# Graph attention and experts on one core: in the edge loop the row of destinations is fetched ahead of the list issues

## The reference

```python
hh = (x @ W).reshape(n, H, D)                       # 8 heads of 32
scores = leaky_relu(s_src[src] + s_dst[dst], 0.2)
e = exp(scores - segment_max(scores, dst)[dst])
alpha = e / segment_sum(e, dst)[dst]
out = segment_sum(hh[src] * alpha[:, :, None], dst) + x
x = x + elu(layernorm(out) * gamma + beta)          # graph part
topk_vals, topk_idx = top_k(layernorm(x) @ gate_w + gate_b, 2)
moe = sum_k softmax(topk_vals)[k] * expert[topk_idx[k]](layernorm(x))
x = x + layernorm(layernorm(x) + moe) * fgamma + fbeta
```

## Time and profile before

| what | value |
|---|---|
| time, median of 3 runs | 3183.66 us (3183.1 to 3186.14) |
| profiled execution: time / its span in the trace | 3181.73 us / 3180.0 us |
| PE busy | 1780.2 us (56%) |
| DVE busy | 1751.1 us (55%) |
| ACT busy | 1115.8 us (35%) |
| POOL busy | 1866.0 us (59%) |
| gathers of the edge loop (L1267) | 1546.6 us busy, 907.1 us idle before them |

### The profile page before, as it was taken

One profiled execution on the slowest core, in us unless ns is written; L12 is line 12 of the kernel. 1 busy time (PEld: TensorE's weight loads), 2 busy tenths in 40 slices (PEclk: granted clock), 3 DMA queues, 4 the chain that ended last, 5 costly groups with the idle time before them and its releaser, 6 DMA issues. The chain is left out here.

```text
span 3180.0 us, 43836 instructions
## 1 busy us (share of the span) xinstructions
PE 1780.2 (56%) x9087; PEld 1452.8 (46%) x9088; DVE 1751.1 (55%) x4247; ACT 1115.8 (35%) x2079; POOL 1866.0 (59%) x1931
## 2 busy tenths in 40 slices
PE   6344445454454545455454545455454545899995
PEld 5233334343343434333343434344343434799994
DVE  6544546464555546455554646454555646665655
ACT  3323233324333333424333332333333332343443
POOL 2356666666666666666666666666666651555553
PEclk9667777786777777786777777686777777999998
DMA  5444343444434344443434344443434346433337
GB/s 189 114 115 112 105 128 106 125 119 116 127 107 128 109 124 118 118 125 107 127 107 129 110 120 115 118 126 109 127 106 129 109 120 182 148 106 103 106 105 249
DMA packets 185064, 393.00 MB, mean 124 GB/s; under 512 B 50817, under 2 KB 107610, under 8 KB 178756
## 3 DMA queue, kind: packets, MB, share of 16 engines
q0 software_dynamic: 90864, 262.34, 29.4%
q1 hardware_dynamic: 71112, 109.44, 11.2%
q10 hardware_dynamic: 23052, 20.83, 2.4%
HBM read 355.94 MB, written 36.52 MB: 123 GB/s over the span
## 5 line engine op out<-in xcount | busy, mean ns | idle before, releaser
L1267 POOL DMA_INDIRECT gat<-table,idx x1627 | 1546.6, 951 | 907.1 <-issue 460.0
L1366 PE MATMUL ps_sum<-msg,hot 128*128 128x264 f32 x3322 | 1096.0, 501 | 672.2 <-DVE msg L1413 397.8
L1366 PEld LDWEIGHTS ps_sum<-msg,hot 128*128 128x128 f32 x3322 | 827.9, 255 | 881.0 <-issue 686.9
L1413 DVE TENSOR_TENSOR msg<-gat,ps_weight 128x2304 f32<-128x2304 f32 x196 | 472.1, 2409 | 585.5 <-ACT ps_weight L1324 381.3
L1279 ACT ACTIVATE hotT<-dst_row,neg_id 128x4352 bf16<-128x4352 int16 x48 | 188.2, 3921 | 534.9 <-DMA dst_row<-dst_half 495.1
L1352 PE MATMUL ps_look<-dst_split,hotT 128*128 (+1 forms) x1661 | 80.6, 192 | 508.1 <-ACT hotT L1281 353.6
L1352 PEld LDWEIGHTS ps_look<-dst_split,hotT 128*128 128x128 bf16 x1661 | 67.2, 102 | 528.6 <-issue 518.6
L1410 DVE TENSOR_TENSOR hot<-ps_own,rel 128x1152 f32<-128x1152 f32 x196 | 250.4, 1277 | 0.0
L1566 DVE TENSOR_TENSOR num<-acc,ps_sum 128x264 f32<-128x264 f32 x49 | 21.0, 429 | 394.7 <-PE ps_sum L1366 202.3
L2056 POOL DMA_INDIRECT chosen<-o_sb,put_at x105 | 121.7, 1160 | 161.0 <-DMA chosen<-o_sb,put_at 71.2
L2130 PE MATMUL ps_ht<-xT,w_t 128*128 128x128 f32 x1712 | 212.9, 278 | 0.0
(11 more groups left out here) (410 smaller groups left out, 2143.7 us busy)
## 6 DMA issues: line engine op xcount, KB each, us to landing
dst_row<-dst_half SPq DMA_DIRECT2D x49, 1088.0 KB
gat<-table,idx POOLq DMA_INDIRECT x1661
b_t<-in_L_ffn_b_dram ACTq DMA_DIRECT2D x107, 128.0 KB
listing<-list_f SPq DMA_DIRECT2D x736, 0.5 KB
table<-rows SPq DMA_DIRECT2D x49, 128.0 KB, 1.7
y_rows<-y SPq DMA_DIRECT2D x48, 128.0 KB
x_all<-in_x_dram SPq DMA_DIRECT2D x6, 896.0 KB, 8.8
w_sb<-in_L_ffn_w_dram SPq DMA_DIRECT2D x2, 2560.0 KB
```

Source lines behind the costliest of these rows:

```text
L1267: pool.indirect_dma_start(gat[:, GSTART[g] + k, :], None, table, bass.IndirectOffsetOnAxis(ap=idx[g][:, k:k + 1], axis=0)).then_inc(landed ...
L1366: made = pe.matmul(ps_sum[:, 0:SUM], hot[:, m, k, :], msg[:, m, k, :], start=(g == 0 and k == 0), stop=(g == NG - 1 and k == n - 1))
L1413: dve.tensor_tensor(msg[:, m, 0:n, 0:D].rearrange("p j (h d) -> p j h d", d=HD), gat[:, j:j + n, 0:D].rearrange("p j (h d) -> p j h d", d=HD),
```

## The change

It touches three orders and two buffers, and leaves all arithmetic as it is.

1. SyncE: in tile t the row of t + 1 is fetched, after the edges of t + 1 and `y` of t - 3, and before the gates and the 16 lists of t - 3. It waits for the first pass of `hotT` of t (`apart_ready`), since `dst_row` has one buffer.
2. ScalarE makes `hotT` of t + 1 after the fourth group's weights, indices and `rel`, as the last work of tile t.
3. TensorE looks up the first group of t + 1 after the fourth sum of t.
4. `base_i` and `list_f` have two halves, chosen by the tile's parity. VectorE waits for the lists of one tile earlier than before; SyncE waits for all earlier lists before it issues sixteen more.

```diff
             def tile(t, head, old, last=False):
-                if not head:
-                    lo = window(t)
-                    sp.wait_ge(hotT_ready, t)
-                    sp.sem_inc(sp_turn, 1)
-                    sp.dma_start(dst_row[:, :], dst_half[bass.ds(lo, WIN)].unsqueeze(0).to_broadcast([P, WIN])).then_inc(row_in, 16)
                 if not last:
                     edges(t + 1)
+                if old >= 3:
+                    finish.keep(sp, t - 3, sp_turn)
+                if not last:
+                    row(t + 1)
                 if old >= 3:
                     finish.record(sp, t - 3, sp_turn)
...
+            def row(t):
+                lo = window(t)
+                sp.wait_ge(apart_ready, t)
+                sp.sem_inc(sp_turn, 1)
+                sp.dma_start(dst_row[:, :], dst_half[bass.ds(lo, WIN)].unsqueeze(0).to_broadcast([P, WIN])).then_inc(row_in, 16)
...
-                    if g == NG - 1 and not last:
-                        rows(t + 1)
                     act.wait_ge(score_ready, t * NG + g + 1)
...
                 if not last:
                     relative(t + 1)
+                    rows(t + 1)
...
                     if g < NG - 1:
                         look(t, g + 1, head, last)
-                    elif not last:
-                        look(t + 1, 0, False)
...
+                if not last:
+                    look(t + 1, 0, False)
...
-        if not (isinstance(a, int) and a == 0):
-            dve.wait_ge(self.listed, a * (16 * EXPERTS))
-        link(dve.tensor_tensor(self.base_i[:, :], self.base[:, :], self.expert_row[:, :], ALU.add))
+        if not (isinstance(a, int) and a < 2):
+            dve.wait_ge(self.listed, (a - 1) * (16 * EXPERTS))
+        link(dve.tensor_tensor(one(self.base_i[:, bass.ds(a & 1, 1), :]), self.base[:, :], self.expert_row[:, :], ALU.add))
...
     def record(self, sp, a, turn):
-        self.keep(sp, a, turn)
         sp.wait_ge(self.list_ready, a + 1)
         sp.sem_inc(turn, 1)
         self.keep_gates(sp, a)
+        if not (isinstance(a, int) and a == 0):
+            sp.wait_ge(self.listed, a * (16 * EXPERTS))
+            sp.sem_inc(turn, 1)
         for e in range(EXPERTS):
-            at = sp.value_load(self.base_i[0:1, e:e + 1], min_val=0, max_val=DROWS - P)
-            sp.dma_start(self.lists[bass.ds(at, P)].unsqueeze(0), self.list_f[e:e + 1, :]).then_inc(self.listed, 16)
+            at = sp.value_load(one(self.base_i[0:1, bass.ds(a & 1, 1), e:e + 1]), min_val=0, max_val=DROWS - P)
+            sp.dma_start(self.lists[bass.ds(at, P)].unsqueeze(0),
+                         one(self.list_f[e:e + 1, bass.ds(a & 1, 1), :])).then_inc(self.listed, 16)
```

More of the change, by code:

```diff
@@ L1506, in __init__ @@
         self.both, self.both_h = sb("both_f", [P, EXPERTS]), sb("both_h", [P, EXPERTS], BF16)
-        self.base, self.base_i = sb("base", [P, EXPERTS]), sb("base_i", [P, EXPERTS], I32)
+        self.base, self.base_i = sb("base", [P, EXPERTS]), sb("base_i", [P, 2, EXPERTS], I32)
         self.base_f, self.at_f, self.at_i = sb("base_f", [P, EXPERTS]), sb("at_f", [P, 2]), sb("at_i", [P, 2], I32)
@@ L1511, in __init__ @@
         self.named, self.spots = sb("named", [P, 2, EXPERTS]), sb("spots", [P, 2, P])
-        self.list_f = sb("list_f", [EXPERTS, P])
+        self.list_f = sb("list_f", [EXPERTS, 2, P])
         self.ready, self.par_in, self.gate_in = sem("finish_consts"), sem("par_in"), sem("gate_in")
@@ L1646, in place, with spots_of_listed @@
                           self.rank[:, :].unsqueeze(2).to_broadcast([P, 2, P]), ALU.is_equal).then_inc(self.entries, 1)
-    def spots_of_listed(self, dve, link):
-        link(dve.tensor_copy(self.base_f[:, :], self.base_i[:, :]))
+    def spots_of_listed(self, dve, link, a):
+        link(dve.tensor_copy(self.base_f[:, :], self.base_i[:, a & 1, :]))
         link(dve.tensor_tensor(self.hit[:, :, :], self.base_f[:, :].unsqueeze(1).to_broadcast([P, 2, EXPERTS]),
@@ L1676, in hand_over @@
         dve.wait_ge(self.list_done, a + 1)
-        dve.tensor_copy(self.list_f[:, :], ps_route[0:EXPERTS, LIST_AT:LIST_AT + P]).then_inc(self.list_ready, 1)
+        dve.tensor_copy(one(self.list_f[:, bass.ds(a & 1, 1), :]), ps_route[0:EXPERTS, LIST_AT:LIST_AT + P]).then_inc(self.list_ready, 1)
     def norm_inner(self, act, a):
@@ L1898, in _ @@
             finish.affine(dve, link, ps_affine)
-            finish.spots_of_listed(dve, link)
+            finish.spots_of_listed(dve, link, a - 1)
             finish.lift(dve, link, b)
```

## The result

The changed kernel takes 3358.15 us (median of 4 runs, 3342.37 to 3364.19) beside 3183.38 us of the kernel before: ratio 1.0536, 95% interval 1.0514 to 1.0559. The forecast was 3171. The profiled execution took 3352.46 us, its span is 3350.6.

What follows compares the result with a forecast made beforehand. It took GpSimd's gathers plus pauses, with TensorE's signals held until GpSimd stops, to bound the edge loop. From the profiled 3181.7 us, -9 (late rows) and -4 (one long pause), plus 1.9 to the median, gave 3171; range 3090 to 3260.

Steps and rivals of the forecast that it cites:

- Which bound holds now: Edge loop: GpSimd's gathers and pauses fill each 50.98 us tile; TensorE's signals wait for its stops; SyncE's ring doesn't pace.
- The row's lateness: Late `dst_row` in the edge loop: fetching it earlier takes tiles from 50.98 to 50.75 us, 9 us in all.
- `hotT`, 3.9 + 3.8 us, then runs under products and sum ... Its price there: nothing: End of each tile on ScalarE: the moved `hotT` ends 37.5 us in, covered with 13 us to spare, costing nothing.
- only once GpSimd has stopped: Edge loop: while gathers run back to back, TensorE's signals reach other engines only after GpSimd stops; pauses 8.4 us a tile.
- stops at the half group 47.4 us in, and the signal follows: GpSimd's fourth group in the early tile: it still stops mid-group, and the sum's signal comes at 50.6 us.
- 38 + 3 + 5 = 46 us of 50.75: covered, by 5: SyncE's work per tile: present work, longer lists and longer creep total 46 us, within the 50.75 us tile.
- The 3 us for the longer list: SyncE's 16 list issues: one more step each costs 1 to 11 us a tile, taken as 3.
- The 5 us for the creep: SyncE's lists: an earlier fourth sum lengthens the slow stretch, losing up to 8 us a tile, taken as 5.
- SyncE becomes the bound: Rival, chance 0.22: SyncE's work grows to 39 to 57 us a tile; 3237 us at 52.3, 3430 at 57.
- signals come through: Rival, chance 0.18: earlier sums signalled before GpSimd's half-group stop; fourth pause goes, 144 us, 3028; at most 346 us.
- My floor of 2838: Lowest time of the 0.18 rival: all 8.4 us of GpSimd's pauses go in 41 tiles, 346 us.
- a behaviour of this loop: Edge loop: no row tells why TensorE's signals are late, so the lateness was taken as belonging to this loop.

Runs made afterwards that it cites:

- hot_late_wait: Parts 2 and 3 alone on the kernel before, plus GpSimd's fourth-group stop also waiting for the next tile's look-up: 3160.72 beside 3181.70 us, 0.9936, held session.
- experiments 6 and 7: In held sessions against the kernel before: parts 2 and 3 alone, 1.0687; the same with GpSimd's added look-up wait, 0.9936; parts 1 and 4 alone, 1.0291.
- experiment 7: Held session, against the kernel before: parts 2 and 3 with GpSimd's added look-up wait, 0.9936; parts 1 and 4 alone, 3275.65 us, 1.0291.
- hot_late_4: The kernel before with parts 2 and 3 alone, run in a held session: 3420.87 beside 3198.25 us, 1.0687.
- after_load3: The changed kernel with three more loads of the list place at each of SyncE's 16 list issues, prompt session: 3316.61 us, 1.2011 against the kernel before.
- hot_late: The kernel before with parts 2 and 3 alone; first run, in a prompt session, 1.0001 against 2758.66 us.

## Why the prediction was wrong

**Which bound holds now** was right. The row's lateness was worth little (14 tiles of the changed kernel with nothing late take 49.7 us, I had said 50.6 to 50.8). The fourth sum starts where I put it: in the tile at 1090.34 TensorE begins it at 1122.97, 32.6 us in (32 said), and `num` follows only at 1139.66. `hot_late_wait` is the nearest that was run to the kernel I had in mind: ScalarE waits 96.8 us for the row from 427 to 2600 us instead of 489.9, GpSimd's pauses are 8.0 us a tile, and the ratio is 0.9936, where 3171 would have been 0.996.

**"`hotT`, 3.9 + 3.8 us, then runs under products and sum ... Its price there: nothing"** is the step that failed most. `hotT` itself is covered. But the look-up had moved with it, behind the fourth sum, and I had just said that signals reach the others only once GpSimd has stopped. I applied that to the sum and not to the look-up that now comes after it. And I had the fourth stop in each tile: "stops at the half group 47.4 us in, and the signal follows". GpSimd stops there only for the sum. Where the sum's signal comes early the stop is short or missing, and the look-up stays in until the gathers next pause, up to 18 us in all. Parts 2 and 3 alone cost 6.9% by this, and one wait takes all of it back (experiments 6 and 7). In the whole change it strikes 13 of 43 tiles; that late edges shift GpSimd's groups against the sum in the others is argued, not shown, and the whole change with the added wait was not run.

**"38 + 3 + 5 = 46 us of 50.75: covered, by 5"** had the right place and a term too small. SyncE took the whole tile of 54 to 55 us and waited for nothing. The 3 us for the longer list are right in a prompt session: 547 against 258 ns an issue, 20.56 us for 15 lists against 14.96 for 13, 1.4 against 1.2 us a list. The 5 us for the creep are not: in the tile shown, 37.57 us of lists and 10.5 to the next edges are 48.1 us, against 27.22 + 5.8 = 33.0 before, 15 more; over all tiles the means are 47.2 and 33.6, 13.6 more where I had 3 + 5. How the held session splits them between list and creep no run shows. I had counted SyncE's idle 13 us as cover, but it lay in the very stretch where its steps take 0.7 us and more, so work put there costs several times its price. Parts 1 and 4 alone cost 2.9% by this (experiment 7). The rival "SyncE becomes the bound", held at 0.22, is this part; at 57 us it reached 3430, and at 55 it gives 3350, beside the measured 3358. The range ended at 3260, since it gave that tail 0.05.

**The rival "signals come through"** has two halves. Its sign, GpSimd's pause in the fourth group gone because the sum was signalled before, is there in eight of the 43 tiles of the changed kernel and in all 38 of `hot_late_4`; so "only once GpSimd has stopped" was too strong. Its gain of 3.5 us a tile is not, since the look-up needed that pause. All pauses went only in the prompt sessions, six of the nine: 2759 us for the kernel before. My floor of 2838 took the pauses from 41 tiles only; all 48 at 8.3 us (50.54 - 42.2) are 398 us, and the first `num` comes 27 us earlier (194.3 against 221.8). I wrote "a behaviour of this loop"; it is one of the machine at the time, which one profile could not tell.

The Trainium skill (Trainium Kernel Development and Optimization, Best Practices) tells to double-buffer and to overlap DMA with compute. By the runs that is worth 14% where SyncE is loaded and signals are prompt (3384.85 to 2908.31), nothing where GpSimd sets the tile (1.0023), and it costs 5% where signals are held.

## What to carry to other kernels

When a signal is seen late, ask which event lets it out, and then put every instruction that somebody waits for ahead of that event, or have the event wait for it. A moved step takes its signal along: check who reads it and when. And idle time of an engine is cover only if its work runs at full speed there.

The best kernel of a held session here is the old SyncE order with the late `hotT`, the late look-up and GpSimd's added wait (0.9936, a gain of 0.6%). It was not run in a prompt session.

## What the runs showed of the hardware that was not expected

The same program on the same chip (number 3) took 2757.6 us in one session and 3181.7 us in another. In a held session TensorE's signals arrive up to 18 us late while gathers run back to back, and 2 to 4 us after they stop, also when GpSimd goes on with fills. They don't all wait for that: `num` at 1442.73 in `hot_late_4` came 7.7 us after its sum (1428.88 + 6.16) with gathers running. SyncE's steps of 0.03 to 0.5 us take 0.7 us and more in the same stretches. In a prompt session neither is seen, with gathers running all through the loop. Gathers themselves take 951 to 954 ns in the one and 947 to 955 in the other. TensorE's mean granted clock does not tell the two apart: it is 0.770 in the changed kernel of the first comparison and 0.770 in `after_load3`, a prompt run with about as long a tile. Only the edge loop differs: from the last `num` to the end of the program it is 3180.0 - 2647.7 = 532.3 us in the held profile of the kernel before and 2755.9 - 2221.9 = 534.0 us in the prompt profile of `hot_late`. What brings the condition about stays open: added small transfers did not. Nor is it shown that signals leave strictly in order, or what lets a sum's signal out while gathers run; that the younger look-up stays behind when the stop for the older sum is short or missing is what the rows show.
